# One launch of attention plus feed-forward on one core: the same calls in another order on all five engines, with filler matmuls at other places

## What is computed

```python
q, k, v = x @ wq, x @ wk, x @ wv                  # one head, DH = 128
q, k = rope(q) / sqrt(DH), rope(k) / sqrt(DH)     # half of the width is rotated
s = q @ k.T - 1e30 * (i < j)                      # causal
x = layernorm(x + softmax(s) @ v @ wo)
h = gelu(x @ (alpha1 * sign(w1)).T + b1)          # 128 -> 512
x = layernorm(x + h @ (alpha2 * sign(w2)).T + b2) # 512 -> 128
```

## Time and profile before

| | |
|---|---|
| median of 3 runs | 276.61 us (275.88 to 279.37) |
| span of the profiled execution | 274.5 us |
| what lies around the span, taken as the difference to the median | 2.1 us |
| PE, DVE, ACT, POOL busy | 260.9, 229.6, 224.7, 167.2 us |

### The profile page before, as it was taken

How to read it: one execution, slowest core, us unless ns; L and a number is a source line. 1 busy time by engine, 2 the same in 40 slices (tenths; PEclk the granted TensorE clock), 3 DMA queues, 4 the chain that set the end, 5 groups by cost and what they waited for, 6 DMA issues and landing times.

```text
span 274.5 us, 5184 instructions
## 1 busy us (share of the span) xinstructions
PE 260.9 (95%) x1485; PEld 208.7 (76%) x1487; DVE 229.6 (84%) x638; ACT 224.7 (82%) x398; POOL 167.2 (61%) x258
## 2 busy tenths in 40 slices
PE   7899999999999999999999999999999999999960
PEld 3678989987779588868879688868886878897630
DVE  2799999999999996999979987998689738537984
ACT  3378964565897989996998999898999799999972
POOL 3033132613625698399821998497819887887772
PEclk9999999999999999999999999999999999999997
DMA  7944596479657936833685318825830720200323
GB/s 178 166 61 87 107 145 98 115 163 192 104 132 160 199 94 153 180 47 78 173 187 127 82 39 249 184 71 151 189 73 27 197 55 2 76 2 0 111 90 108
DMA packets 58012, 31.94 MB, mean 116 GB/s; under 512 B 33408, under 2 KB 54400, under 8 KB 57984
## 3 DMA queue, kind: packets, MB, share of 16 engines
q1 hardware_dynamic: 57024, 30.76, 50.4%
q10 hardware_dynamic: 960, 0.85, 1.3%
HBM read 9.18 MB, written 4.19 MB: 49 GB/s over the span
## 4 chain that ended last, share of the span: by engine, by line
PE 81%; DVE 6%; ACT 5%; issue 3%; DMA 2%; ACTq 1%; POOL 0%; POOLq 0%
PE pair L589 18%; PE bank L606 18%; PE bank L632 5%; PE bank L674 4%; PE pair L650 4%; PE pair L651 4%; PE bank L620 4%; PE bank L682 4%; PE bank L683 4%; PE bank L719 2%; DMA sin_sb<-in_sin_dram 2%; PE pair L663 2%; PE pair L665 2%; PE pair L664 2%; PE bank L639 2%
## 5 line engine op out<-in xcount | busy, mean ns | idle before, releaser
L391 POOL TENSOR_TENSOR hid_lo<-hid,hid_hi 128x1024 fp32r<-128x1024 f32 x28 | 66.0, 2386 | 19.7 <-ACT hid_hi L1075 19.7
L1004 ACT ACTIVATE prob<-pair,negmax 128x128 f32<-128x128 f32 (+3 forms) x64 | 47.2, 742 | 14.2 <-DVE negmax L1457 12.5
L606 PE MATMUL bank<-probT,xa 128*128 128x512 f32 (+3 forms) x160 | 54.2, 482 | 0.0
L1457 DVE CUSTOM_DVE_ANT_0 pair<-pair,mask_row 128x128 f32<-128x128 f32 (+3 forms) x64 | 47.9, 759 | 6.1 <-PE pair L589 5.5
L606 PEld LDWEIGHTS bank<-probT,xa 128*128 128x128 f32 x160 | 29.1, 190 | 20.2 <-issue 15.3
L341 POOL TENSOR_TENSOR xT_lo<-xT,xT_hi 128x512 fp32r<-128x512 f32 x14 | 18.0, 1288 | 40.4 <-ACT xT_hi L1034 40.4
L1467 DVE STREAM_TRANSPOSE turned<-prob 128x128 f32<-128x128 f32 (+7 forms) x56 | 39.5, 724 | 0.5 <-ACT prob L1004 0.5
L589 PE MATMUL pair<-qkT_hi 128*128 128x512 f32 (+3 forms) x96 | 36.0, 375 | 0.8 <-DVE qkT_lo L1619 0.3
L1068 ACT ACTIVATE hid<-pair,b_sb,alpha 128x1024 f32<-128x1024 f32 x28 | 32.9, 1209 | 0.1
L589 PE MATMUL pair<-qkT_lo,qkT_hi 128*128 128x512 f32 (+3 forms) x96 | 32.8, 342 | 0.0
L589 PE MATMUL pair<-qkT_hi,qkT_lo 128*128 128x512 f32 (+3 forms) x96 | 32.8, 342 | 0.0
(11 more groups left out here) (116 smaller groups left out, 649.9 us busy)
## 6 DMA issues: line engine op xcount, KB each, us to landing
probT<-turned SPq DMA_DIRECT2D x96, 116.0 KB, 2.3
probT<-turned SPq DMA_DIRECT2D x128, 52.0 KB, 2.0
xq<-in_L_attn_x_dram SPq DMA_DIRECT2D x28, 128.0 KB, 4.0
xa<-in_L_attn_x_dram SPq DMA_DIRECT2D x7, 512.0 KB, 4.7
out_dram<-res SPq DMA_DIRECT2D x7, 512.0 KB, 3.3
hid<-in_L_ffn_w_dram SPq DMA_DIRECT2D x2, 256.0 KB, 3.2
out_dram<-res SPq DMA_DIRECT2D x2, 256.0 KB, 2.3
xa<-in_L_attn_x_dram SPq DMA_DIRECT2D x1, 256.0 KB, 3.6
```

Source lines behind the costliest of these rows:

```text
L391: pool.tensor_tensor(hid_lo[:, j, :], hid[:, j, :], hid_hi[:, j, :].bitcast(F32), ALU.subtract).then_inc(s_hid_lo[j], 1)
L606: ins = pe.matmul(bank_of["px", g, c][:, 0:n * P], xa[c % 2][:, j, :], probT[g][:, :, TG * j:TG * j + n, :].rearrange("p n m i -> p m n i" ...
L1004: act.activation(prob[r % 3][:, 0:(r + 1) * P], pair_of["score", r, c][:, slice(*columns(r))], ACT.Exp, scale=-1.0, bias=negmax[:, r:r + 1 ...
L1457: dve.tensor_tensor_reduce(mine, mine, mask_row[:, T - (r + 1) * P:T], -1.0, -MASKED, ALU.add, ALU.min, negmax[:, r:r + 1]).then_inc(s_max ...
```

## The change

It changes the order of the calls on all five engines. On PE the fillers are now 8 (`keep_warm`), then `fill(6)` ahead of the first transposes, `fill(3)` and `fill(2)` ahead of the first projection, `fill(4)` after the first two `turn_qk`, and one `fill(2)` near the end: 25 in all. `fill` waits for a pair only if three have been used before. The semaphores `s_px` are two (one for each group) in place of eight, of which two were used; who waits for what is the same. All other calls are the same, each once. ScalarE's table loads stay 14.

```diff
-            sems("s_qk", NG), sems("s_qkT", 4), sems("s_score", NT), sems("s_px", NT), sems("s_attn", NG))
+            sems("s_qk", NG), sems("s_qkT", 4), sems("s_score", NT), sems("s_px", NG), sems("s_attn", NG))
...
-                wait_freed(*list(pair_of)[-len(pairs)])
+                if len(pair_of) >= len(pairs):
+                    wait_freed(*list(pair_of)[-len(pairs)])
...
             keep_warm(8)
+            fill(6)
             turn_x0(0)
             turn_x0(1)
-            keep_warm(4)
+            fill(3)
+            fill(2)
             project(0, 0)
             project(1, 0)
-            keep_warm(3)
             turn_qk(0, 0)
             turn_qk(1, 0)
-            keep_warm(6)
+            fill(4)
             setup_turn_wv()
             scores(0, 0)
+            setup_wvo()
             scores(1, 0)
-            fill(2)
...
             x0T_low(0)
             x0T_low(1)
+            x_squares(0, 1)
+            x_squares(1, 1)
             rotate(0, 0)
             first_rotation_sum(0)
             rotate(1, 0)
-            x_squares(0, 1)
             qkT_low(0, 0)
             qkT_low(1, 0)
+            setup_wvT()
             first_rotation_sum(1)
-            setup_wvT()
             row_max(0, 0)
+            x_squares(0, 2)
             row_max(1, 0)
-            x_squares(1, 1)
```

More of the change, by code:

```diff
@@ L272, in _ @@
             carry(1, 3)
+            carry(0, B - 4)
             stripes(B - 1)
-            carry(0, B - 4)
             tokens(B - 4)
@@ L609, in weigh_group @@
                 if last == rows[-1]:
-                    ins.then_inc(s_px[last], 1)
+                    ins.then_inc(s_px[g], 1)
             def weigh_row(r, c):
@@ L901, in _ @@
             scores(7, B - 2)
+            weigh_group(1, 0, 3, B - 3)
+            weigh_group(1, 4, 7, B - 3)
             turn_x1(1, B - 4)
-            weigh_group(1, 0, 3, B - 3)
+            project(1, B - 1)
             turn_qk(0, B - 1)
-            weigh_group(1, 4, 7, B - 3)
+            turn_qk(1, B - 1)
             up(0, B - 4)
             up(1, B - 4)
-            turn_qk(1, B - 1)
-            project(1, B - 1)
             project_out(1, B - 3)
@@ L961, in _ @@
             weigh_row(7, B - 1)
+            up(3, B - 2)
+            turn_y(1, B - 3)
             turn_x1(0, B - 1)
+            fill(2)
             project_out(1, B - 1)
@@ L1655, in _ @@
             qkT_low(0, 1)
-            x_squares(0, 2)
-            x_squares(1, 2)
+            row_copy(5, 0)
             qkT_low(1, 1)
-            reciprocals(1, 0)
-            row_copy(5, 0)
             row_copy(6, 0)
             row_copy(7, 0)
+            rotate(0, 2)
             row_max(0, 1)
+            qkT_low(2, 1)
+            reciprocals(1, 0)
+            turn_row(0, 1)
             row_max(1, 1)
-            qkT_low(2, 1)
-            qkT_low(3, 1)
-            rotate(0, 2)
-            row_max(2, 1)
-            turn_row(0, 1)
-            turn_row(1, 1)
             x_squares(0, 3)
             x_squares(1, 3)
+            qkT_low(3, 1)
+            row_max(2, 1)
             row_max(3, 1)
+            turn_row(1, 1)
             turn_row(2, 1)
@@ L1676, in _ @@
             turn_row(3, 1)
-            row_max(5, 1)
-            turn_row(4, 1)
             residual1(0, 0)
@@ L1734, in _ @@
             first_norm(7, 0)
-            statistics1(0, 1)
+            residual1(0, 1)
+            residual1(1, 1)
+            residual1(2, 1)
+            residual1(3, 1)
+            x1T_low(0, 0)
+            turn_row(3, 2)
             turn_row(4, 2)
+            x1T_low(1, 0)
+            row_max(6, 2)
+            reciprocals(0, 2)
             row_max(7, 2)
-            x1T_low(1, 0)
+            rotate(1, 3)
+            qkT_low(0, 3)
             turn_row(5, 2)
             turn_row(6, 2)
-            reciprocals(0, 2)
-            statistics1(1, 1)
-            statistics1(2, 1)
-            statistics1(3, 1)
             turn_row(7, 2)
@@ L1850, in _ @@
             x1T_low(1, 2)
+            rotate(0, B - 2)
             residual1(4, 3)
@@ L1899, in _ @@
             statistics1(3, B - 4)
-            statistics2(0, 1)
-            turn_row(4, B - 3)
-            turn_row(5, B - 3)
-            turn_row(6, B - 3)
-            x1T_low(1, 3)
-            x_squares(1, B - 1)
-            rotate(1, B - 2)
-            qkT_low(0, B - 2)
-            qkT_low(1, B - 2)
             residual1(4, B - 4)
-            turn_row(7, B - 3)
             residual1(5, B - 4)
@@ L1913, in _ @@
             residual1(7, B - 4)
-            statistics2(1, 1)
+            rotate(0, B - 1)
+            qkT_low(2, B - 2)
             statistics1(4, B - 4)
```

775 lines of the change are left out of this document (388 added, 387 removed).

## The result

The changed kernel takes 299.19 us (median of 4 runs, 298.9 to 302.79), the kernel before 276.55 us in the same session (275.88 to 279.37). The ratio is 1.084, with a 95% interval of 1.076 to 1.092. The forecast was 280.3 us with a range to 284.0: it is wrong by 18.9 us, and by far the most of that is one kind of instruction that the prediction never priced.

A forecast was written before the change was run, and what follows sets the result against it. The prediction saw PE, DVE and SP as three full queues in lockstep until about 100 us. It summed 274.5 + 4.5 - 0.3 - 0.5 = 278.2, plus 2.1 from profiled execution to median: 280.3 us, range 275.0 to 284.0.

The forecast's parts named there:

- Step 1: Start of DVE: two `x_squares` wait for chunk 1's stripes until 11.5 us, so `rotate(0, 0)` starts 3.9 us late.
- Step 2: DVE near the start: `first_rotation_sum(1)` no longer stalls beside POOL's `xT_low(0, 1)`, 1.1 us taken back.
- Steps 3 and 4: `turn_row(3, 0)` ends 3.3 us late; chunk 3's `x_squares` wait again; `carry(0, 1)` comes 4.5 us late.
- Step 5: PE's `weigh_group(0, 0, 3, 1)` up to 3.9 us late; no slack at `weigh_group(1, 0, 3, 2)`, so 4.5 us carried to the end.
- absorbed: Rival: PE works on while DVE and SP are late and keeps 1.5 us of debt; 277.3 us, chance 0.23.
- Step 6: Rest of the kernel: front fillers 0, fewer fillers near the end 0.3 us gained, PE's body waits 0.5 us gained.
- The terms 0.3 and 0.5: Gains in us: 0.3 from seven fewer fillers near the end, 0.5 from PE's remaining waits in the body.
- The clock falls in the gap: Rival: PE idles 4.1 us before `turn_qk(0, 0)` and its clock halves; 281.6 us, or 284 to 287; chance 0.17.
- the short dip: Half clock only just behind PE's early gap, about 1.3 us lost; 281.6 us, two thirds of the 0.17.
- Faster: Rival: chunk 1's stripes land before DVE asks, so the `x_squares` fill its idle 1.44 us; 273.4 us, chance 0.10.

The follow-up runs named there:

- b_ahead: The old kernel with the two `x_squares` of chunk 1 moved ahead of `rotate(0, 0)` and nothing else: 280.48 us.
- a_free: The changed kernel with `first_norm` in the form that also writes its accumulator to a spare tile: 278.6 us.
- a_free_front2: The changed kernel with `first_norm` in accumulator form and the front put back (early `x_squares`, `xT_high(0, 1)`, fillers almost as before): 275.74 us.
- after: The changed kernel itself, with no further edit: 299.19 us.
- a_front2: The changed kernel with plain `first_norm` and the front put back (early `x_squares`, `xT_high(0, 1)`, fillers almost as before): 298.15 us.
- b_collide: The old kernel with three `first_norm` of chunk 1 moved a few calls later, into POOL's run of `hidden_low`: 283.49 us.
- b_collide_free: The old kernel with the same three `first_norm` moved into POOL's run of `hidden_low`, and `first_norm` in accumulator form: 276.76 us.
- a_free_bridge: The changed kernel with `first_norm` in accumulator form and 15 fillers between `project(1, 0)` and `turn_qk(0, 0)`: 277.95 us.
- a_clear: The changed kernel with plain `first_norm`, its late instances of chunks 1 to 5 moved earlier on DVE: 301.08 us.

## Why the prediction was wrong

**Step 1, the first wait: right.** `rotate(0, 0)` at 12.77 (forecast 12.8), behind two `x_squares` that waited for `xq` until 11.54 (11.5). Made in the old kernel, it costs 4.1 us (b_ahead).

**Step 2, the stall that goes: right.** `first_rotation_sum(1)` took 0.68 us at 18.33. The mechanism was the one that decided the whole case, and I applied it to this one operation only.

**Steps 3 and 4: right, a little high.** `turn_row(3, 0)` ended at 23.7 (23.4), the second pair of waiting `x_squares` ended at 40.9 (41.4), `carry(0, 1)` began at 44.8 (45.4). `turn_row(3, 0)` was 0.3 us later than forecast, but the 16 issues of `carry(0, 0)` took 10.1 us this time, not 10.84, which accounts for the lower numbers behind it.

**Step 5, what PE sees: right in kind, too large.** `weigh_group(0, 0, 3, 1)` came at 56.85, 2.3 us late instead of 3.9, and `weigh_group(1, 0, 3, 2)` at 93.35, 2.4 late instead of 4.5. The front measured by itself is worth 2.6 to 2.9 us (a_free to a_free_front2), the half clock in its gap included, where the sum carried 4.5 to the end without it. That lies between the forecast and the rival "absorbed" (1.5). Why PE got back the rest was not tried.

**Step 6, the rest: this is the step that failed.** It put the body at 0.5 us gained, "from 1.3 gained to 3 lost", and so took every duration of DVE as fixed in a new order. What the runs showed in its place: 19 `first_norm` that took up to 2.43 us in place of 0.34. This lock-out was worth 20.6 us (after to a_free), or 22.4 with the front put back (a_front2 to a_free_front2). Without it, and with the front put back, the new order is 0.8 us faster than the old (275.74 to 276.52, by its interval between 0 and 1.1). The terms 0.3 and 0.5 came to the same; neither was measured, so this may be luck. In the forecast's own terms: 276.5 - 0.8 + 2.9 + 20.6 = 299.2, which adds up by construction, as each term is the difference of two of these runs.

The clue was in the trace of before. `first_norm` had 64 instances with minimum 306 and maximum 436 ns:

```profile
L1499 DVE TENSOR_SCALAR x<-res,ln x64: 306/342/436, 56.2 to 253.1; 128x128 f32<-128x128 f32 x64
```

The one of 436 ns, at 225.90, ended 0.08 us after a `hidden_low`, and `hidden_low` took 2.39 us, 28 times, in the same part of the program. The Trainium skill (SBUF — State Buffer, "Who interferes with whom") lists `tensor_scalar`, "not the form that also writes out its accumulator", among the operations of DVE that can enter a mode in which they contend with GpSimd for a shared port pair, if their operands allow it, and says that the one that comes second "fully blocks". The runs agree on both halves: 2.37 us for the plain form, 0.40 us for the other at the same place (b_collide, b_collide_free). By that rule the count to make was: which DVE operations of this form stand, in the new order, within a run of POOL instructions. At up to 2 us each (2.37 - 0.34) for 4 instances in each of 7 chunks my estimate of the bound is 56 us. Nothing in the prediction's range allowed for a cost of this kind.

**The rivals.** "The clock falls in the gap" happened, as the short dip: half from 15.6 to 19.0 us and full again. It costs little, by a_free_bridge 0.4 to 0.65 us, not settled, against 1.3. It is not why the kernel is slow. A second dip at 247.7 to 254.5 begins in the 3.7 us that PE waits for the eight `first_norm` at 242.24; in a_free, without the lock-out, it is not there. "Absorbed" held in part. "Faster" fell with the landing at 11.5.

**What stays open.** Both DVE's and POOL's lists changed, and no run has one of them alone. So it is shown that the plain `first_norm` in POOL's run of `hidden_low` is the cost, and not which of the two lists carries more of the blame. That it is the port pair and nothing else between the two engines is the account of the Trainium skill; the runs show only that the stall ends with one POOL instruction and is absent in the other form. Why POOL's power of 1.04 us held no `first_norm` is open.

## What to carry to other kernels

When only an order changes, the durations are not given: list the DVE operations from SBUF to SBUF that can be held up by a GpSimd operation, and look at what stands beside them before and after. A short DVE operation can cost its neighbour's length, not its own; the form with an accumulator output took the risk away here at 0.06 us each and a read of 0.08 us, and made the fast order and the slow order differ by 2.0 us instead of 22.6. To undo an early wait, follow it through to the next instruction that can wait for the same queue: putting back the first pair alone only moved the idle time.

## What the runs showed of the hardware that was not expected

- A 128x128 fp32 `tensor_scalar` of 0.34 us lasted up to 2.43 us beside POOL subtractions of 2.37 us, in a row as often as POOL had one ready (9.45 us for four). POOL's own durations hardly changed: a mean of 2373 to 2390 ns in all the kernels that have `hidden_low` whole. Each long instance of after ended 0.08 or 0.09 us after a POOL subtraction.
- Being recorded inside a POOL instruction is not enough: in after, four `first_norm` ran at 0.31 to 0.34 us inside a 1.04 us power of POOL on a 128x4 tile (two of them at 149.74).
- In a_clear the first of the four is recorded as starting at 124.35 us, before POOL's at 124.43, and still lasted 2.53 us. So the recorded start doesn't tell who is held up: by it, the one that came second, and had to wait, would have been POOL.
- One block of 6.70 us on DVE, 5.7 us more than the three need, cost 7.0 us of the kernel, with a wait of PE of 5.1 us and a stretch at half clock in it; 24.1 us more, spread over the kernel, cost 20.6.
- Cutting POOL's instruction in two is cheap: 1.28 us for each half against 2.37 for the whole, 0.2 us more.
